# A turn ahead of the second pair of scores, behind the weighted sum, in a gated attention and expert kernel

## The chip, the core and the metric

The kernel runs on one core of one Trainium2 chip. The metric is the device time of one execution in microseconds, smaller is better. The engines are TensorE (PE in the rows, with PEld for its weight loads), VectorE (DVE), ScalarE (ACT), GpSimdE (POOL) and SyncE (SP). Each works through its own queue in the order of the program and waits for the others at semaphores.

## What is computed

Eight sequences of 512 tokens, 256 wide, attend to 1601 context rows with 16 heads of width 16; then each token goes through two of eight experts. The softmax of the attention runs over the queries, not over the context (`axis=2`), and the second division is by the sum over the context.

```python
def _L0_xattn_ref(q, k, v, Wq, Wk, Wv, Wo):
    scale = Dm ** (-0.5)
    qh, kh, vh = ...                        # heads of q @ Wq.T, k @ Wk.T, v @ Wv.T
    attn = jnp.einsum('bhnc,bhlc->bhnl', qh * scale, kh)
    attn = jax.nn.softmax(attn, axis=2)
    attn = attn / jnp.sum(attn, axis=-1, keepdims=True)
    out = jnp.einsum('bhnl,bhlc->bhnc', attn, vh)
    out = out.transpose(0, 2, 1, 3).reshape(Bq, Nq, Dm)
    return out @ Wo.T

x = x + jnp.tanh(g_xattn[0]) * _L0_xattn_ref(_layernorm(x, axis=-1), ctx_1024, ctx_1024, ...)
x = x + jnp.tanh(g_ffn[0]) * _L0_ffn_ref(_layernorm(x, axis=-1), router_w, w1, w2)
```

## The kernel before

**Stages.** A short start fills the first projections. Then eight attention batches follow one another from about 31 us to 1230 us of the span, and the expert stage takes the rest. The change touches the attention alone.

**Steps.** A batch has 52 steps (`STEPS`): four groups of four heads, by 13 tiles of up to 128 context rows (`LT`). A step `s` has two pairs of heads. For each pair TensorE makes two score tiles of 128x512 (`unit_scores(b, s, 0)` and `unit_scores(b, s, 1)`, L732), VectorE takes the negated maximum of both in one reduction (`negmax`, L1114), and ScalarE takes two exponentials with their sums (L934). I write scores(48,1) for the second pair of step 48, and the same for maxima and exponentials. The scores of a pair go into one of three slots of PSUM (`SLOTS`), so a pair has to wait for the exponentials of the pair three before it. Once the sums of a step are there, VectorE takes a reciprocal (L1100), GpSimdE scales the values (`vz`, L1337), and TensorE makes the weighted sum of the step three before the current one (`weigh(it.b, s - LAG)`, L745, four products of 32x512 that run side by side and add up in `acc`).

**Fills.** Between these, TensorE does the other work of the previous, current and next batch in pieces, one at certain steps, by the table `FILL_AT` (two more tables hold for the first and the last batch). Each piece goes into the one PSUM bank `spare`, and another engine takes it from there. Some are projections (`k`, `q`, `v`, `out_proj`) that are made in two halves, the first half at the step ahead of the table's. Others are turns, which are four transposes of 128x128 each: `o_turn` (L669), `attn_turn` (L672), `row_turn` (L684) and `x_turn` (L582). A piece waits until the one before it has left `spare` (`fill_taken`). VectorE takes `o_turn` with a reciprocal and a product (L1015, L1017) and `attn_turn` and `row_turn` with a copy (L1004); ScalarE takes `x_turn` (L883). VectorE's order within a step is written out: the maximum of the first pair, the taking of a turn, the maximum of the second pair, then the accumulator's copy if one is due (L1104), and the reciprocal of the step before.

**The order on TensorE.** In `run` of the TensorE block a step goes either of two ways. In the ordinary one the fill stands between the first and the second pair, and the weighted sum comes last. Where `begins_behind(s)` holds, which it does where the first half of a piece falls on the step behind another piece's end, the weighted sum goes ahead of the second pair, and the half behind it. The pads and prefixes of the routing and its small steps on VectorE do not matter here.

Of the kernel before, what the change touches and what calls it, by code (L numbers as in the profile page):

```python
# [78 lines left out]
    47: ("next", "v", 6), 48: ("cur", "attn_turn", 0), 49: ("cur", "o_turn", 2),  # L79
}  # L80
LAST_BATCH_FILL_AT = {**FILL_AT, 44: ("tail", "pads", 0)}
HALVED = ("k", "q", "v", "own_v", "out_proj")
LAST_V = (("v", VF - 1), ("own_v", VF - 1))

# [29 lines left out]
class Iteration:  # L114


    def __init__(self, b, tail=True, cur=True, nxt=True):
        self.b, self.tail, self.cur, self.next = b, tail, cur, nxt
        has = {"tail": tail, "cur": cur, "next": nxt}
        self.ahead = nxt and not (b + 2 >= B)  # L120
        self.table = FIRST_BATCH_FILL_AT if b == 0 else LAST_BATCH_FILL_AT if b == B - 1 else FILL_AT
        order = [self.table[s] for s in sorted(self.table) if has[self.table[s][0]]]
# [14 lines left out]
    def halves(self, s):  # L137

        now, after = self.fill(s), self.fill(s + 1)
        begun = after and after[0] in HALVED and after not in LAST_V  # L140
        assert not (begun and now) or now[0] in HALVED
        if now:
            split = now[0] in HALVED and now not in LAST_V
            return [(now, (1,) if split else (0, 1))]
        return [(after, (0,))] if begun else []

    def begins_behind(self, s):

        begun = any(halves == (0,) for _, halves in self.halves(s))
        return begun and self.fill(s - 1) is not None and (s - LAG) % LT > 0  # L150

    def chunk(self, name, i):
# [21 lines left out]
def wait(eng, sem, value):  # L174

    if not (isinstance(value, int) and value <= 0):
        eng.wait_ge(sem, value)
# [30 lines left out]
def rows_of(lt):  # L208
    return min(P, L - lt * P)


def attention_and_routing(nc, ctx, block, keep, x, ctx_t, g_xattn, g_ffn, wq_t, wk_t, wv_t, wo_t, router_t,
# [203 lines left out]
    def stacks_by(b, g):  # L416

        return b * LOADS - (LOADS if b > 0 and g == 0 else 0)
# [160 lines left out]
    def _(pe):  # L579
        def turn_x(bank, i):  # L580
            for t in range(NT):
                mm = pe.transpose(bank[:, t * P:(t + 1) * P], x_in[:, t, i * P:(i + 1) * P], ident[:, :])  # L582
            return mm

        def project_q(bank, i, halves):
            for k in halves:
                mm = pe.matmul(bank[:, :], wq_sb[:, k, i * P:(i + 1) * P], x_t[:, k, :], start=(k == 0), stop=(k == KC - 1))
            return mm

        def project_k(bank, i, halves):  # L590
            m, c = i // KCHUNK, i % KCHUNK
            for k in halves:
                mm = pe.matmul(bank[:, 0:KCOLS[c + 1] - KCOLS[c]], wk_sb[:, k, m * P:(m + 1) * P],  # L593
                               ctx_sb[:, k, KCOLS[c]:KCOLS[c + 1]], start=(k == 0), stop=(k == KC - 1))
            return mm

        def project_v(bank, i, halves):
            for lt in (2 * i + h for h in halves if 2 * i + h < LT):
                r = rows_of(lt)
                for k in range(KC):  # L600
                    mm = pe.matmul(bank[0:r, (lt % 2) * D:(lt % 2 + 1) * D], ctx_sb[:, k, lt * P:lt * P + r],  # L601
                                   wv_sb[:, k, :], start=(k == 0), stop=(k == KC - 1))
            return mm
# [39 lines left out]
        def fill(it, name, i, halves):  # L643
            b = it.b
            if 0 not in halves:
                pass
            elif name != "logits":

                wait(pe, fill_taken, it.made(name, i) - 1)
            if name == "x_turn":  # L650

                pe.wait_ge(xn_ready, 2 * (b + 2))
                mm = turn_x(spare, i)
            elif name == "q":
                mm = project_q(spare, i, halves)
            elif name == "k":
                if i == 0 and 0 in halves:
                    pe.wait_ge(ctx_loaded, (b + 1) * 16)
                mm = project_k(spare, i, halves)
            elif name in ("v", "own_v"):  # L660
                if (name, i) == ("own_v", len(EARLY_COPIED) - KC) and 0 in halves:

                    pe.wait_ge(early_copied, len(EARLY_COPIED))
                mm = project_v(spare, i, halves)
            elif name == "o_turn":

                pe.wait_ge(acc_taken, b * G + i + 1 if i < G - 1 else b * G)
                for t in range(NT):
                    mm = pe.transpose(spare[:, t * P:(t + 1) * P], o_acc[:, t * P:(t + 1) * P], ident[:, :])  # L669
            elif name == "attn_turn":  # L670
                for t in range(NT):
                    mm = pe.transpose(spare[:, t * P:(t + 1) * P], attn[:, t, i * P:(i + 1) * P], ident[:, :])  # L672
            elif name == "out_proj":
                if i == 0:
                    pe.wait_ge(wo_in, 32)
                for t in (2 * i + h for h in halves):
                    for k in range(KC):
                        mm = pe.matmul(spare[:, (t % 2) * D:(t % 2 + 1) * D], attn_t[:, k, t * P:(t + 1) * P],
                                       wo_sb[:, k, :], start=(k == 0), stop=(k == KC - 1))
            elif name == "row_turn":  # L680

                pe.wait_ge(rows_ready, 2 * b)
                for t in range(NT):
                    mm = pe.transpose(spare[:, t * P:(t + 1) * P], routed_rows[:, 0, t, i * P:(i + 1) * P], ident[:, :])  # L684
            elif name == "logits":
                for t in range(NT // 2, NT):
                    for k in range(KC):
                        mm = pe.matmul(spare[:, t * E:(t + 1) * E], row_t[:, k, t * P:(t + 1) * P],
                                       router_sb[:, k, :], start=(k == 0), stop=(k == KC - 1))
            elif name == "pads":  # L690
                mm = pe.matmul(spare[:, 0:E], ones[:, :], seen[:, :], start=True, stop=True)
            else:

                pe.wait_ge(route_step, b * ROUTE_STEPS)
                pe.matmul(spare[:, 0:NT * E], tri[:, :], chosen[:, :, :], start=True, stop=False)
                mm = pe.matmul(spare[:, 0:NT * E], ones[:, :], seen_at[:, :, :], start=False, stop=True)
            if 1 in halves:
                mm.then_inc(fill_ready, 1)
# [9 lines left out]
        def unit_scores(b, s, p):  # L708
            u = 2 * s + p
            g, lt = s // LT, s % LT  # L710
            if lt == 0 and p == 0:

                wait(pe, stack_in[g], stacks_by(b + 1, g))
                if b == 0 and g == 0:
                    pe.wait_ge(early_q_in, 16 * BLOCKS)
                    pe.wait_ge(early_k_in[0], 16 * BLOCKS)
            if b == 0 and g == 0 and p == 0 and lt == HALFWAY // P:
                pe.wait_ge(early_k_in[1], 16 * BLOCKS)

            emptied = 2 * (b * UNITS + (u - SLOTS if u >= SLOTS else (-2, -1, -3)[u]))  # L720
            if b == 0 and u < SLOTS:

                held = EARLY[u * 2 + 1 + BANKS_EARLY]
                if held in EARLY_SPLIT:
                    pe.wait_ge(early_split, EARLY_SPLIT.index(held) + 1)
                else:
                    pe.wait_ge(early_copied, EARLY_COPIED.index(held) + 1)
            for j in (2 * p, 2 * p + 1):
                r = rows_of(lt)

                wait(pe, exp_done, emptied + j % 2 + 1)
                mm = pe.matmul(scores[0:r, 2 * (u % SLOTS) + j % 2, :], k_stacks[g][:, j, lt * P:lt * P + r],  # L732
                               q_stack[:, g, j, :], start=True, stop=True)
            mm.then_inc(scores_ready, 1)
# [14 lines left out]
        def run(it):  # L749
            for s in range(STEPS):  # L750
                late = s >= LAG and it.cur and it.begins_behind(s)
                if it.cur:
                    unit_scores(it.b, s, 0)
                if late:
                    weigh(it.b, s - LAG)
                    unit_scores(it.b, s, 1)
                for f, halves in it.halves(s):
                    fill(it, *f, halves)
                if it.tail and s == LOGITS - 1:
                    first_logits(it)  # L760
                if it.cur and not late:
                    unit_scores(it.b, s, 1)
                    if s >= LAG:
                        weigh(it.b, s - LAG)
                if s < LAG and it.tail:
                    weigh(it.b - 1, STEPS + s - LAG)
# [63 lines left out]

        first()
        over_batches(pe, run)
        last()

# [854 lines left out]
```

## Time and profile before

| | |
|---|---|
| median of 3 runs | 1798.06 us (1796.43 to 1799.73) |
| the profiled execution's own time | 1794.36 us |
| its span in the profile | 1792.6 us |
| PE / DVE / ACT busy over the span | 95% / 79% / 72% |
| one attention batch, start to start | 151.3 us |
| busy in one such batch: ACT, DVE, PE | 148.63, 144.83, 143.79 us |

The shares over the whole span mix two stages: in the expert stage ScalarE has little to do and TensorE is the engine in front. In the attention all three are nearly full, so the question there is which one waits last, and that is read in the timeline, step by step. The granted TensorE clock is 1.00 of full speed in every attention batch. A busy ACT hides short stalls: the row of an exponential also covers the time in which it stood queued, and the distance between two starts tells more. It is 0.66 us where nothing holds ScalarE.

### The profile page before, as it was taken

What the parts mean: (1) busy time and instruction counts of PE and PEld (TensorE: products, weight loads), DVE (VectorE), ACT (ScalarE), POOL (GpSimd) and SP (SyncE); (2) the same over time, 40 slices, a digit from 0 to 9 for tenths busy, and PEclk for the clock granted to TensorE, in tenths of its full rate; (3) what the DMA queues carried; (4) which work ended last, traced back from release to release, by engine and by line L of the source; (5) the groups of instructions that cost most, each with busy time, mean ns of one, the idle gap of its engine ahead of it and who ended that gap; (6) DMA issues with size and microseconds to landing.
All of it is one profiled execution on the core that took longest, in us unless ns stands there. A gap on an engine that the chain in (4) does not pass through costs nothing.

```text
span 1792.6 us, 31795 instructions
## 1 busy us (share of the span) xinstructions
PE 1703.8 (95%) x10074; PEld 918.3 (51%) x10074; DVE 1417.2 (79%) x2293; ACT 1283.0 (72%) x3653; POOL 538.2 (30%) x821
## 2 busy tenths in 40 slices
PE   8999999999999999999999999889999999999997
PEld 5233334333333433333333342225899999999997
DVE  7998999999999999999999999997344444444442
ACT  5999999999999999999999999996111111111111
POOL 3331252352343225235223422213122222222222
PEclk9999999999999999999999999999999999999999
DMA  8546226414712721551371163419222222222221
GB/s 231 139 121 183 66 70 158 129 40 123 187 47 62 198 72 52 158 154 40 102 187 51 51 172 75 154 52 326 67 37 35 36 37 35 38 35 35 36 37 27
DMA packets 128247, 172.90 MB, mean 96 GB/s; under 512 B 14496, under 2 KB 105760, under 8 KB 128128
## 3 DMA queue, kind: packets, MB, share of 16 engines
q1 hardware_dynamic: 113152, 150.51, 30.8%
q0 software_dynamic: 14144, 20.44, 6.6%
q8 instruction: 54, 0.88, 0.2%
q14 instruction: 65, 0.53, 0.1%
q10 hardware_dynamic: 832, 0.53, 0.1%
HBM read 117.96 MB, written 53.47 MB: 96 GB/s over the span
## 4 chain that ended last, share of the span: by engine, by line
ACT 40%; PE 30%; DVE 20%; issue 7%; DMA 2%; POOL 1%; SPq 0%; POOLq 0%; DVEq 0%; ACTq 0%
ACT w_all L934 37%; DVE negmax L1114 14%; PE scores L1507 14%; PE scores L1520 13%; ACT w_all L879 1%; ACT parts L870 1%; DVE resid L1009 1%; DMA out<-row_t,gate_token 1%; PE spare L1497 1%; DVE rz L1100 1%; PE scores L732 1%; PE spare L593 1%; DVE x L1025 1%; DVE stats L1133 1%; DVE stats L1143 0%
## 5 line engine op out<-in xcount | busy, mean ns | idle before, releaser
L934 ACT ACTIVATE w_all<-scores,negmax 128x512 f32<-128x512 f32 (+1 forms) x1664 | 1128.9, 778 | 19.9 <-DVE negmax L1114 15.4
L1114 DVE TENSOR_REDUCE negmax<-scores 128x2 f32<-128x1024 f32 (+1 forms) x832 | 1001.9, 1215 | 53.8 <-PE scores L732 47.4
L732 PE MATMUL scores<-q_stack,w_all 128*128 128x512 bf16 (+1 forms) x1664 | 532.9, 385 | 42.1 <-ACT w_all L934 34.3
L934 ACT ACTIVATION_READ_ACCUMULATOR w_all<-scores,negmax 128x1 f32 (+1 forms) x1664 | 495.2, 298 | 0.0
L745 PE MATMUL acc<-w_all,vz 128*32 128x512 f32 (+1 forms) x3328 | 443.7, 605 | 0.0
L732 PEld LDWEIGHTS scores<-q_stack,w_all 128*128 128x128 bf16 (+1 forms) x1664 | 136.8, 99 | 575.2 <-ACT w_all L934 514.6
L1553 ACT ACTIVATE projections<-scores 128x512 f32<-128x512 f32 x142 | 84.8, 597 | 445.8 <-PE scores L1507 440.2
L1337 POOL TENSOR_TENSOR vz<-w_all,rz 128x68 f32<-128x68 f32 (+1 forms) x416 | 124.5, 299 | 776.3 <-DVE rz L1100 751.0
L1507 PEld LDWEIGHTS scores<-row_t,q_stack 128*128 128x128 f32 x2272 | 264.4, 192 | 7.0 <-issue 2.0
L1507 PE MATMUL scores<-row_t,q_stack 128*128 128x128 f32 x2272 | 265.6, 275 | 1.9 <-DVE row_t L1580 1.9
L1520 PE MATMUL scores<-room,projections 128*128 128x256 f32 x1136 | 256.8, 379 | 0.0
L1633 POOL DMA_INDIRECT out<-row_t,gate_token x71 | 120.3, 1694 | 407.9 <-DVE row_t L1593 374.3
L1520 PEld LDWEIGHTS scores<-room,projections 128*128 128x128 f32 x1136 | 210.4, 190 | 25.7
L1586 DVE COPY gate_token<-parts 128x2 f32<-128x2 f32 x71 | 12.0, 169 | 186.3 <-DMA out<-row_t,gate_token 186.3
L745 PEld LDWEIGHTS acc<-w_all,vz 128*32 128x32 f32 (+1 forms) x3328 | 65.6, 108 | 138.1 <-issue 121.9
L593 PE MATMUL spare<-w_all,projections 128*128 128x400 f32 (+1 forms) x228 | 97.7, 511 | 10.2 <-DVE resid L1009 10.2
L1593 DVE TENSOR_SCALAR row_t<-scores,gate_token 128x256 f32<-128x256 f32 x71 | 34.4, 484 | 88.0 <-PE scores L1520 88.0
L601 PE MATMUL spare<-projections,w_all 128*128 128x256 f32 (+1 forms) x400 | 103.1, 381 | 0.1
L1570 DVE COPY q_stack<-w_all 128x2048 f32 x71 | 86.9, 1225 | 6.4 <-issue 1.8
L1575 DVE COPY room<-w_all 128x2048 f32 x71 | 86.5, 1218 | 0.0
L601 PEld LDWEIGHTS spare<-projections,w_all 128*128 128x128 f32 (+1 forms) x400 | 73.6, 186 | 19.8 <-ACT w_all L879 3.3
L1100 DVE RECIPROCAL rz<-z 128x4 f32<-128x4 f32 (+1 forms) x416 | 69.7, 167 | 2.1 <-ACT w_all L934 2.1
(215 smaller groups left out, 1048.9 us busy)
## 6 DMA issues: line engine op xcount, KB each, us to landing
w_all<-k_parts SPq DMA_DIRECT2D x248, 200.1 KB, 3.5
w_all<-in_w SPq DMA_DIRECT2D x16, 1024.0 KB, 10.0
q_stack<-q_parts SPq DMA_DIRECT2D x248, 64.0 KB, 3.3
k_parts<-parts SPq DMA_DIRECT2D x42, 300.0 KB, 2.9
w_all<-in_ctx_t SPq DMA_DIRECT2D x7, 1601.0 KB, 7.1
parts<-routed SPq DMA_DIRECT2D x71, 129.0 KB
q_parts<-parts SPq DMA_DIRECT2D x14, 384.0 KB, 3.9
routed<-pad_row SPq DMA_DIRECT2D x8, 645.0 KB
```

The source lines that it names most:

```text
L593: mm = pe.matmul(bank[:, 0:KCOLS[c + 1] - KCOLS[c]], wk_sb[:, k, m * P:(m + 1) * P], ctx_sb[:, k, KCOLS[c]:KCOLS[c + 1]], start=(k == 0), ...
L601: mm = pe.matmul(bank[0:r, (lt % 2) * D:(lt % 2 + 1) * D], ctx_sb[:, k, lt * P:lt * P + r], wv_sb[:, k, :], start=(k == 0), stop=(k == KC ...
L732: mm = pe.matmul(scores[0:r, 2 * (u % SLOTS) + j % 2, :], k_stacks[g][:, j, lt * P:lt * P + r], q_stack[:, g, j, :], start=True, stop=True)
L745: mm = pe.matmul(acc[32 * j:32 * j + 32, :], vz[0:r, s % RING, j, :], probs[0:r, s % RING, j, :], start=(lt == 0), stop=(lt == LT - 1))
L934: act.activation(probs[0:r, s % RING, j, :], scores[0:r, 2 * (u % SLOTS) + j % 2, :], ACT.Exp, bias=negmax[0:r, u % 4, j % 2:j % 2 + 1], a ...
L1100: dve.reciprocal(rz[0:r, s % RING, :], z[0:r, s % RING, :]).then_inc(rz_ready, 1)
L1114: dve.tensor_reduce(negmax[0:r, u % 4, :], scores[0:r, 2 * (u % SLOTS):2 * (u % SLOTS) + 2, :], AX.X, ALU.max, negate=True).then_inc(negma ...
L1337: pool.tensor_tensor(vz[0:r, s % RING, :, 0:DH + 1], v_ones[b % 2][0:r, lt, g * GH:(g + 1) * GH, :], rz[0:r, s % RING, :].unsqueeze(2).to_ ...
L1507: mm = pe.matmul(ps_hidden[:, slot * BANKS + h // HB, (h % HB) * BLK:(h % HB + 1) * BLK], w1_sb[:, slot, k * HID + h * P:k * HID + (h + 1) ...
L1520: mm = pe.matmul(ps_y[:, slot, 0:D], hidden[:, slot, h * BLK:(h + 1) * BLK], w2_sb[:, slot, h * D:(h + 1) * D], start=(h == 0), stop=(h == ...
L1570: dve.tensor_copy(w1_sb[:, slot, :], w1_all[:, bass.ds(e * (KC * HID), KC * HID)]).then_inc(w1_ready, 1)
L1633: pool.indirect_dma_start(out=out, out_offset=bass.IndirectOffsetOnAxis(gate_token[:, slot, 1:2].bitcast(U32), 0), in_=result[:, slot, :], ...
```

## The change

A turn that stands directly behind another piece's step is now a reason for the second order too, and in such a step the turn goes behind the weighted sum and ahead of the second pair. At the old places of the second order, where no fill ends in the step, nothing changes: the second pair still goes ahead of the half.

```diff
+TURNS = ("o_turn", "attn_turn", "row_turn", "x_turn")
...
-        begun = any(halves == (0,) for _, halves in self.halves(s))
+        begun = any(halves == (0,) or f[0] in TURNS for f, halves in self.halves(s))
         return begun and self.fill(s - 1) is not None and (s - LAG) % LT > 0
...
                 if late:
                     weigh(it.b, s - LAG)
-                    unit_scores(it.b, s, 1)
+                    if not it.fill(s):
+                        unit_scores(it.b, s, 1)
                 for f, halves in it.halves(s):
                     fill(it, *f, halves)
+                if late and it.fill(s):
+                    unit_scores(it.b, s, 1)
```

This meets 70 steps: in each of the six middle batches steps 4, 5, 18, 19, 20, 27, 28, 33, 48 and 49; in the first batch 18, 27, 28, 33, 44 and 48; in the last one 5, 19, 20 and 49. No instruction is added or removed, and only TensorE's queue changes. The line numbers behind L146 move by one, so L732 becomes L733, and behind L753 by up to four.

On TensorE, steps 48 and 49 of the second batch before the change (L732 is a pair of scores, L745 a weighted sum, L672 and L669 the two turns):

```order
L732 MATMUL scores<-q_stack,w_all 128x512 x2
L672 MATMUL spare<-ident,room 128x128 x4
L732 MATMUL scores<-q_stack,w_all 128x512 x2
L745 MATMUL acc<-w_all,vz 32x512 x4
L732 MATMUL scores<-q_stack,w_all 128x512 x2
L669 MATMUL spare<-ident,o_acc 128x128 x4
L732 MATMUL scores<-q_stack,w_all 128x512 x2
L745 MATMUL acc<-w_all,vz 32x512 x4
```

And the same two steps after it, where L733, L746, L673 and L670 are the same four lines:

```order
L733 MATMUL scores<-q_stack,w_all 128x512 x2
L746 MATMUL acc<-w_all,vz 32x512 x4
L673 MATMUL spare<-ident,room 128x128 x4
L733 MATMUL scores<-q_stack,w_all 128x512 x4
L746 MATMUL acc<-w_all,vz 32x512 x4
L670 MATMUL spare<-ident,o_acc 128x128 x4
```

The weighted sum has moved ahead of the turn, and the second pair of a step now stands next to the first pair of the following one.

On TensorE, steps 18 and 19 of the same batch before (L669 is the `o_turn`, L684 the `row_turn`):

```order
L732 MATMUL scores<-q_stack,w_all 128x512 x2
L669 MATMUL spare<-ident,o_acc 128x128 x4
L732 MATMUL scores<-q_stack,w_all 128x512 x2
L745 MATMUL acc<-w_all,vz 32x512 x4
L732 MATMUL scores<-q_stack,w_all 128x512 x2
L684 MATMUL spare<-ident,routed_rows 128x128 x4
```

And after (L670 and L685 are the turns):

```order
L733 MATMUL scores<-q_stack,w_all 128x512 x2
L746 MATMUL acc<-w_all,vz 32x512 x4
L670 MATMUL spare<-ident,o_acc 128x128 x4
L733 MATMUL scores<-q_stack,w_all 128x512 x4
L746 MATMUL acc<-w_all,vz 32x512 x4
L685 MATMUL spare<-ident,routed_rows 128x128 x4
```

The same move: the turn that VectorE takes next stands one weighted sum further back. VectorE's, ScalarE's and GpSimdE's own rows are the same as before.

## Rows read from the trace of the kernel before

**Rows 1.** Busy time by engine in the fifth batch's stretch; us, instructions in brackets

```profile
634.49:785.79 151.30, 143.79 (x797) 51.21 (x797) 144.83 (x234) 148.63 (x436) 54.25 (x94) 1.00 0.39 108
```

**Rows 2.** Groups by line over six batches: count | busy us, mean ns | idle before

```profile
L934 ACT ACTIVATE w_all<-scores,negmax 128x512 f32<-128x512 f32 (+1 forms) x1249 | 848.0, 761 | 16.0 <-DVE negmax L1114 11.8
L1114 DVE TENSOR_REDUCE negmax<-scores 128x2 f32<-128x1024 f32 (+1 forms) x625 | 753.1, 1214 | 38.6 <-PE scores L732 34.6 <-issue 0.6
```

**Rows 3.** Timeline, steps 48 and 49 of the fifth batch: start us, duration us, instruction

```profile
771.84 0.61 PE L732 MATMUL scores<-q_stack,w_all 128*128 128x512 bf16 x2
...
772.28 0.60 PE L672 MATMUL spare<-ident,room 128*128 128x128 f32 x4
...
772.48 1.23 DVE L1114 TENSOR_REDUCE negmax<-scores 128x2 f32<-128x1024 f32 x1 [0.23 <-PE scores L732]
...
773.62 0.68 DVE L1004 COPY room<-spare 128x512 f32<-128x512 f32 x1
...
773.77 1.06 PE L745 MATMUL acc<-w_all,vz 128*32 128x512 f32 x8
...
774.77 0.60 PE L732 MATMUL scores<-q_stack,w_all 128*128 128x512 bf16 x2
...
776.55 0.25 DVE L1015 RECIPROCAL rden<-spare 128x16 f32<-128x16 f32 x1
...
777.18 1.22 DVE L1114 TENSOR_REDUCE negmax<-scores 128x2 f32<-128x1024 f32 x1
...
778.42 0.87 ACT L934 ACTIVATE w_all<-scores,negmax 128x512 f32<-128x512 f32 x1
```

**Rows 4.** Timeline of TensorE's weight loads at the attention's end

```profile
1228.07 0.16 PEld L745 LDWEIGHTS acc<-w_all,vz 128*32 128x32 f32 x8 [0.95 <-POOL vz L1337]
1229.07 0.52 PEld L780 LDWEIGHTS spare<-router_sb,ones 128*128 128x128 f32 x4 [0.84 <-issue]
```

**Rows 5.** Timeline, step 18 of the fifth batch

```profile
685.61 0.60 PE L732 MATMUL scores<-q_stack,w_all 128*128 128x512 bf16 x2
...
686.57 0.66 PE L669 MATMUL spare<-ident,o_acc 128*128 128x128 f32 x4 [0.36 <-DVE resid L1009]
...
687.06 0.59 PE L732 MATMUL scores<-q_stack,w_all 128*128 128x512 bf16 x2
...
687.56 0.25 DVE L1015 RECIPROCAL rden<-spare 128x16 f32<-128x16 f32 x1
687.59 0.16 PEld L745 LDWEIGHTS acc<-w_all,vz 128*32 128x32 f32 x8 [0.42 <-issue]
...
689.44 0.69 ACT L934 ACTIVATE w_all<-scores,negmax 128x512 f32<-128x512 f32 x1 [0.25 <-DVE negmax L1114]
```

**Rows 6.** Timeline, step 4 of the fifth batch

```profile
643.99 0.61 PE L732 MATMUL scores<-q_stack,w_all 128*128 128x512 bf16 x2
...
646.20 0.25 DVE L1015 RECIPROCAL rden<-spare 128x16 f32<-128x16 f32 x1
```

**Rows 7.** Timeline, step 33 of the fifth batch

```profile
728.40 0.60 PE L732 MATMUL scores<-q_stack,w_all 128*128 128x512 bf16 x2
...
730.84 0.24 DVE L1015 RECIPROCAL rden<-spare 128x16 f32<-128x16 f32 x1
```

**Rows 8.** Timeline, step 27 of the fifth batch, first scores and the second pair's exponential

```profile
710.58 0.61 PE L732 MATMUL scores<-q_stack,w_all 128*128 128x512 bf16 x2
...
715.20 0.79 ACT L934 ACTIVATE w_all<-scores,negmax 128x512 f32<-128x512 f32 x1
```

**Rows 9.** Timeline, step 44 of the first batch

```profile
155.19 0.60 PE L732 MATMUL scores<-q_stack,w_all 128*128 128x512 bf16 x2
...
156.98 0.25 DVE L1015 RECIPROCAL rden<-spare 128x16 f32<-128x16 f32 x1
```

**Rows 10.** Timeline, step 19 of the last batch

```profile
1138.68 0.60 PE L732 MATMUL scores<-q_stack,w_all 128*128 128x512 bf16 x2
...
1140.75 0.68 DVE L1004 COPY row_t<-spare 128x512 f32<-128x512 f32 x1
```

## The prediction

> **What bounds the kernel now.** I read the stretches by batch first, then the groups by line, then the timeline at the steps that the change meets. A middle batch lasts 151.30 us, and ScalarE is busy in 148.63 of it, VectorE in 144.83, TensorE in 143.79 [rows 1]. So ScalarE sets the pace, with 2.67 us to spare, and the two engines that feed it are almost as full. The groups say what it waits for: of 16.0 us idle before the exponentials of six batches, 11.8 ended with a maximum from VectorE [rows 2]. VectorE waits for scores, 34.6 us in the same six batches, and much of that costs nothing, since three slots of scores let it lag.
>
> The timeline shows which of these matters at a turn. VectorE's work runs back to back: in steps 48 and 49 the maximum from 772.48, the copy at 773.62, the reciprocal at 776.55 and the maximum from 777.18 stand in a chain without idle time (only the first row shows any, 0.23 us for the scores), and the exponential at 778.42 starts 0.02 us behind the end of the last, at 778.40 [rows 3]. At step 18 the exponential says it itself, 0.25 us idle until the maximum [rows 5]. So **at a step with a turn VectorE is the bound, and ScalarE waits for it**. Before the change VectorE never waits for a turn: neither the copies nor the reciprocals that take one show idle time ahead of them [rows 3, 5].
>
> **What the change does to that.** It takes nothing away. It moves the weighted sum ahead of the turn. Two things get later, the turn's result and the scores of the second pair, and one gets earlier, the first pair of the next step, which no longer has a weighted sum directly ahead of it.
>
> *How late the turn is.* I count from the first product of scores(s,0). The turn follows it at once by 0.44 us (771.84 to 772.28) and lasts 0.60, so its result is there at 1.04 [rows 3]. Now: a weighted sum starts 0.53 us behind its pair (687.06 to 687.59) [rows 5]. What follows a weighted sum starts its loads 1.00 us later, for scores (773.77 to 774.77) and for other f32 products alike (1228.07 to 1229.07) [rows 3, 4]. A turn whose first load isn't hidden lasts 0.66 us [rows 5]. And VectorE starts some 0.04 us behind a product's end: the scores at 771.84 last to 772.45, the maximum starts at 772.48 [rows 3]. Together 0.53 + 1.00 + 0.66 + 0.04 = 2.23; the finer starts of these rows make 2.22, and I take that.
>
> *When VectorE wants it.* That is the distance from scores(s,0) to the taking, in the rows of before. What lies between it and 2.22 is the delay, and since VectorE's chain behind it has no idle time before an exponential that already waits, the delay passes through to ScalarE.
> - Step 48, middle batches: 773.62 - 771.84 = 1.78, so the copy comes 0.44 late [rows 3]. The chain from there to the exponential at 778.42 has no gap, so it costs 0.44. Step 49's turn is then ready in time: scores(49,0) moves to some 774.2 (its own slot is emptied later, by 774.8, which holds the next weighted sum back), the turn is there at about 776.8, and VectorE wants it at 776.55 + 0.44.
> - Step 18: 687.56 - 685.61 = 1.95, late by 0.27, and the exponential at 689.44 already waits, so it costs 0.27 [rows 5]. Here the sum also fills the 0.36 us for which TensorE now waits for `spare`, which is why the turn is not later still. Steps 19 and 20 follow while VectorE is behind; their turns are ready 0.5 us before it wants them. Nothing more.
> - Step 4: 646.20 - 643.99 = 2.21, late by 0.01 [rows 6]. Step 5 follows VectorE's backlog, with 0.5 us to spare: 0.
> - Step 33: 730.84 - 728.40 = 2.44, ready 0.22 early: 0 [rows 7].
> - Steps 27 and 28: ScalarE takes these turns, and late. What counts is scores(27,1). It is done 2.02 + 0.60 us behind scores(27,0), so at 713.20; its maximum ends at 714.45, and the exponential isn't due before 715.20 [rows 8]. Margin 0.75: 0. Step 28 has about as much.
>
> The middle batches repeat to 0.01 us, so they give 6 x (0.44 + 0.27 + 0.01) = **4.3 us**.
>
> - The first batch: step 18 as above, 0.26. Step 44, wanted at 1.79, is 0.43 late [rows 9]; its exponential follows the maximum with 0.16 us of margin in the timeline, so 0.27 (0.43 at most). Step 48 has the distances of rows 3 and nearly no margin: 0.38. Together 0.9.
> - The last batch: step 19, wanted at 2.07, is 0.15 late [rows 10]; step 49, wanted at 2.04, 0.18; both are ahead of exponentials that already wait. Step 5 is covered by 0.1, and step 20 follows 19's lag. Together 0.3.
>
> *What gets earlier.* TensorE's queue is as long as before; at a step with a turn, 0.53 + 1.00 + 0.49 + 0.43 us against 0.44 + 0.49 + 0.53 + 1.00. The first pair of the next step comes earlier by at most a few tenths of a microsecond, until its slot is free. That helps only where VectorE waits for just these scores. Of its waits, behind all 70 steps, that is 0.8 us in sum, and these stand where ScalarE has margin. I take 0, with 0.8 us as the end on the side of a gain. Nothing else queues behind the moved sum: it waits for `vz` of three steps before, which GpSimdE has made a step earlier, and ScalarE and VectorE need its result a step later than they get it. No DMA moves.
>
> The sum is 4.3 + 0.9 + 0.3 = **+5.5 us**. Against the profiled execution's own 1794.36 that makes 1799.9; its time lies 3.7 us below the median of the three runs, 1798.06, and the forecast stands on the median: **1803.6 us**.
>
> **A rule against this sum.** The rows show no load between a weighted sum's last load and the next thing's, 0.84 us, whether scores or f32 products follow [rows 4]. The Trainium skill (TensorE: Matmul & The Clock Gate, section "Step-by-step: what each phase is for") says that TensorE may pull weight loads ahead of products in flight where row groups don't conflict or the load goes to the background buffer. By that rule the turn's load would lie under the sum; rows 4 disagree for what follows a weighted sum, and no row shows a turn in that place. It is the first rival below, and its price is from rows alone.
>
> **The rivals.**
> - *The turn starts as soon as the sum has streamed.* The eight products of a weighted sum last 1.06 us, and products of 512 columns that follow one another overlap by some 0.17 us, so a turn with its load hidden would start at 0.88 instead of 1.00 and last 0.60 instead of 0.66: ready at 2.04. Step 48 then costs 0.26, step 18 0.09, step 4 nothing: 6 x 0.35 = 2.1, and the ends 0.4. That is +2.5, or **1800.6 us**, within 0.2%. For it: loads do run ahead elsewhere (a turn directly behind scores lasts 0.60). Against it: both kinds of followers in the rows.
> - *The turn is later than I take it.* At a further 0.2 us, by which the steps at 48, 18 and 4 all grow and 33 stays just covered (margin 0.22), the sum is 6 x (0.64 + 0.47 + 0.21) + 1.5 + 0.7, so +10.1, or **1808.2 us**. For it: no row shows transposes behind a sum of four side by side. Against it: loads for f32 products start on time there.
> - *The other side: scores of the next step decide.* If VectorE's chain is longer only because the next first pair comes late, the change gains. It would decide from the point where VectorE idles ahead of the first maximum behind a turn step. The upper end of that is the 0.8 us above, so **1797.3 us**; for more, ScalarE's 16.0 us of idle time would have to hang on these scores [rows 2], and the rows show VectorE busy without a gap where they would have to show it waiting. A real gain of more than 0.2% by it has hardly a chance.
> - *The loss is given back.* A stall that ScalarE has later in the batch could shrink. Its biggest ones, around steps 0 and 12, follow from ScalarE's own exponentials and slots and so move along. **1798.1 us** if they all did.
> - That the change does nothing at all is excluded: the moved rows stand in TensorE's queue at 70 steps.
>
> **How the numbers follow.** "Faster" and "slower" begin at 0.2%, 3.6 us, about what a measurement of this kernel can tell from none. The forecast has 0.70, the early turn 0.13, the later turn 0.09, the loss given back 0.05, the gain 0.03. A spread of some 1.5 us of the runs lies on each, by the three runs shown. Slower is 0.70 + 0.09 less a tail of the forecast that stays under 3.6 us, 0.02, so 0.77. Same is 0.13 + 0.05 + 0.02, less 0.01 that falls out on the side of a gain, 0.19. Faster is 0.03 and that 0.01, 0.04. The range goes from 1799.9, most of the way to the early turn, to 1808.0, near the later one.
>
> **What would show it.** In the profile of the changed kernel VectorE's copy L1004 and reciprocal L1015 show idle time ahead of them that a turn ended: about 0.44 at step 48 and 0.27 at step 18 of each middle batch, some 5 us in all. A middle batch lasts 152.0 instead of 151.3 us, all of it at exponentials (18,1), (48,1) and (49,1). The turn's loads start 1.0 us behind the sum's. ScalarE's idle time ended by maxima grows. The expert stage stays as it is. I am wrong if the copy at step 48 starts as before relative to scores(48,0), if a middle batch stays at 151.3, or if exponentials of steps 27, 28 or 33 begin to wait.

## The result: slower by 0.14%, less than half of what was forecast

| | before | after |
|---|---|---|
| median of 20 runs each, us | 1796.64 (1792.31 to 1799.73) | 1798.38 (1795.59 to 1803.21) |
| the profiled execution's span, us | 1792.6 | 1795.7 |
| the fifth batch, start to start, us | 151.30 | 151.83 |

The ratio is 1.0014, 95% interval 1.0008 to 1.0021. That is +2.5 us, from +1.4 to +3.8; the two medians alone are 1.7 us apart. It is a loss, as forecast, but of less than the 0.2% from which I called it slower, and the median lies below my range of 1799.9 to 1808.0. A second set of runs of the same kernel gave nearly the same ratio: 1.0015, interval 1.0007 to 1.0024, which is +2.7 us, from +1.3 to +4.3.

The groups by line of the changed kernel, over the whole span (count | busy us, mean ns | idle before), against [rows 2], which is over six batches:

```profile
L938 ACT ACTIVATE w_all<-scores,negmax 128x512 f32<-128x512 f32 (+1 forms) x1664 | 1129.4, 761 | 20.8 <-DVE negmax L1118 15.4
L1118 DVE TENSOR_REDUCE negmax<-scores 128x2 f32<-128x1024 f32 (+1 forms) x832 | 1000.8, 1214 | 52.0 <-PE scores L733 46.4
```

ScalarE's idle time ended by maxima is 15.4 us, and so it was before the change, over the whole span. The equal totals hide two changes. Over the six middle batches it grew from 11.8 to 12.9 us, as forecast, and in the last batch it fell from 1.8 to 0.6, since TensorE's clock had fallen there in the profile of before (a wait of 1.22 us at the first exponential of step 1) and not in this one. The line that shows the cause is in the view of waits (engine, line waited for: us in total, times, longest), and it has no counterpart before:

```profile
DVE room L1008 <- PE spare L673: 2.5, 7, 0.4
DVE rden L1019 <- PE spare L670: 1.7, 8, 0.4
```

VectorE now waits for turns, 15 times (the shortest waits, in the last batch, don't enter this view). The copy L1008 waits at step 48 of seven batches, 0.36 us each. The reciprocal L1019 waits at step 18 of seven batches and once at step 44 of the first. The timeline of steps 48 and 49 of the fifth batch, where [rows 3] had none of it:

```profile
773.82 0.60 PE L733 MATMUL scores<-q_stack,w_all 128*128 128x512 bf16 x2
...
774.36 1.07 PE L746 MATMUL acc<-w_all,vz 128*32 128x512 f32 x8
...
775.35 0.66 PE L673 MATMUL spare<-ident,room 128*128 128x128 f32 x4
...
776.04 0.69 DVE L1008 COPY room<-spare 128x512 f32<-128x512 f32 x1 [0.36 <-PE spare L673]
...
777.87 1.19 DVE L1118 TENSOR_REDUCE negmax<-scores 128x2 f32<-128x1024 f32 x1
777.90 0.72 ACT L938 ACTIVATE w_all<-scores,negmax 128x512 f32<-128x512 f32 x1
```

From the first scores at 773.82 the turn's load comes at 1.53 and the copy at 2.22, as worked out; before the copy stood at 1.78. And step 18, where [rows 5] had the reciprocal 1.95 us behind the scores:

```profile
688.76 0.42 PEld L670 LDWEIGHTS spare<-ident,o_acc 128*128 128x128 f32 x4 [0.84 <-DVE resid L1013]
688.77 0.66 PE L670 MATMUL spare<-ident,o_acc 128*128 128x128 f32 x4
...
689.46 0.26 DVE L1019 RECIPROCAL rden<-spare 128x16 f32<-128x16 f32 x1 [0.19 <-PE spare L670]
...
691.35 0.69 ACT L938 ACTIVATE w_all<-scores,negmax 128x512 f32<-128x512 f32 x1 [0.52 <-DVE negmax L1118]
```

ScalarE's idle time there went from 0.25 to 0.52 us. So the turn is late as forecast, and ScalarE waits for it at step 18. What remained was why a whole batch is only 0.53 us longer when the terms made 0.72, and the kernel +2.5 instead of +5.5.

**A finer reading.** I laid the exponentials of both traces over each other, one by one, from the first of their batch. By their starts the fifth batch falls behind at (18,1) by 0.27 us, (48,1) by 0.19 and (49,1) by 0.22, in sum 0.69, and gets 0.19 back at the very next batch's first exponential. By their ends the loss at (48,1) is 0.00 and that at (49,1) 0.25. There is also a gain of 0.10 at step 12. So starts and ends tell different stories, and the experiments had to say which counts. The exponentials (48,1) and (49,1), before and then after the change:

```profile
775.71 0.92 ACT L934 ACTIVATE w_all<-scores,negmax 128x512 f32<-128x512 f32 x1
778.42 0.87 ACT L934 ACTIVATE w_all<-scores,negmax 128x512 f32<-128x512 f32 x1
```

```profile
777.90 0.72 ACT L938 ACTIVATE w_all<-scores,negmax 128x512 f32<-128x512 f32 x1
780.85 0.69 ACT L938 ACTIVATE w_all<-scores,negmax 128x512 f32<-128x512 f32 x1
```

Both start later within their batch and are recorded as shorter by 0.20 and 0.18 us. I use one measure for the experiments: the length of a middle batch, the distance between the first exponentials of two batches in a row. It repeats within about 0.02 us inside an execution, so it tells apart what the timed runs cannot.

### The profile page after: what moved, and what is told of

The parts are those of the page before. It is cut to its first block, busy times and chain, and to the rows that moved or that the text cites. A ratio compares the mean times of both kernels' runs of the same rounds, so it can differ in the third digit from the quotient of the medians.

```text
span 1795.7 us, 31682 instructions
## 1 busy us (share of the span) xinstructions
PE 1694.8 (94%) x9961; PEld 919.5 (51%) x10074; DVE 1417.1 (79%) x2293; ACT 1285.1 (72%) x3653; POOL 539.7 (30%) x821
## 4 chain that ended last, share of the span: by engine, by line
ACT 35%; PE 34%; DVE 21%; issue 7%; DMA 2%; POOL 1%; SPq 0%; POOLq 0%; DVEq 0%; ACTq 0%
ACT w_all L938 33%; DVE negmax L1118 14%; PE scores L1511 14%; PE scores L1524 13%; PE acc L746 2%; PE scores L733 2%; ACT w_all L883 1%; PE spare L594 1%; ACT parts L874 1%; DVE resid L1013 1%; PE spare L1501 1%; DVE rz L1104 1%; DVE stats L1147 1%; DVE x L1029 1%; DVE stats L1137 1%
## 5 line engine op out<-in xcount | busy, mean ns | idle before, releaser
L938 ACT ACTIVATE w_all<-scores,negmax 128x512 f32<-128x512 f32 (+1 forms) x1664 | 1129.4, 761 | 20.8 <-DVE negmax L1118 15.4
L733 PE MATMUL scores<-q_stack,w_all 128*128 128x512 bf16 (+1 forms) x1551 | 502.1, 384 | 69.4 <-ACT w_all L938 53.7
L938 ACT ACTIVATION_READ_ACCUMULATOR w_all<-scores,negmax 128x1 f32 (+1 forms) x1664 | 466.7, 280 | 0.0
L746 PE MATMUL acc<-w_all,vz 128*32 128x512 f32 (+1 forms) x3328 | 443.0, 605 | 0.0
L733 PEld LDWEIGHTS scores<-q_stack,w_all 128*128 128x128 bf16 (+1 forms) x1664 | 143.0, 99 | 565.1 <-ACT w_all L938 509.9
L746 PEld LDWEIGHTS acc<-w_all,vz 128*32 128x32 f32 (+1 forms) x3328 | 65.6, 108 | 133.2 <-issue 119.7
```

The lines of the kernel that those rows point to most:

```text
L746: mm = pe.matmul(acc[32 * j:32 * j + 32, :], vz[0:r, s % RING, j, :], probs[0:r, s % RING, j, :], start=(lt == 0), stop=(lt == LT - 1))
L938: act.activation(probs[0:r, s % RING, j, :], scores[0:r, 2 * (u % SLOTS) + j % 2, :], ACT.Exp, bias=negmax[0:r, u % 4, j % 2:j % 2 + 1], a ...
```

## The experiments

All kernels are the changed one with an edit to the rule or the order. For the six that only limit the steps, the rule gets one more condition, and `turned` names the steps, given below for the middle, the first and the last batch:

```diff
-        begun = any(halves == (0,) or f[0] in TURNS for f, halves in self.halves(s))
+        turned = s in (... if 0 < self.b < B - 1 else ... if self.b == 0 else ...)
+        begun = any(halves == (0,) or (f[0] in TURNS and turned) for f, halves in self.halves(s))
```

Two theories stood against each other. **The late turn:** VectorE waits for the turn, since a weighted sum is ahead of it. **The late second pair:** the scores of the second pair start later too, 2.24 us behind those of the first pair at step 48 instead of 0.94, and 2.03 instead of 1.45 at step 18, and VectorE or ScalarE waits for them. The traces at hand already speak against the second: over the six middle batches VectorE idles 33.2 us for scores before the change and 34.0 after it.

| kernel | middle batch, us | against 151.30 | ratio to before (95%) |
|---|---|---|---|
| after | 151.83 | +0.53 | 1.0014 (1.0008 to 1.0021) |
| e0_after_again | 151.75 | +0.45 | 1.0015 (1.0007 to 1.0024) |
| e1_covered | 151.52 | +0.22 | 1.0006 (0.9997 to 1.0015) |
| e2_exposed | 151.91 | +0.61 | 1.0022 (1.0011 to 1.0033) |
| e3_turn_sum_pair | 153.09 | +1.79 | 1.0064 (1.0051 to 1.0077) |
| e4_turn_last | 153.19 | +1.89 | 1.0071 (1.0049 to 1.0093) |
| e6_48_only | 151.54 | +0.24 | one run |
| e7_49_only | 151.55 | +0.25 | one run |
| e8_4_and_5 | 151.20 | -0.10 | 0.9995 (0.9986 to 1.0005) |
| e9_18_and_44 | 151.58 | +0.28 | one run |

The batch lengths leave out batches in which TensorE's clock fell, which have a paragraph of their own below.

**e0_after_again**, the changed kernel itself.

> The changed kernel itself once more. By the ends of the exponentials a middle batch is longer by 0.53 us (0.27 at step 18, 0.25 at step 49, less 0.10 around step 12), and that repeats. The first stage and the expert stage carry the rest of any difference between two profiles, up to a microsecond or so. If the time moves as the batches say, the attention brings 4.0 us: 6 x 0.53, some 0.4 for the first batch and 0.35 for the last one. The rival is that the batches' difference comes and goes from one execution to the next; then its middle batches are not 151.83 us.

Measured: 151.75 us, and nearly the same ratio. The terms repeat: by the ends of the exponentials +0.28 at step 18, -0.09 at step 12, and +0.26 at step 49, where the first trace has +0.25. In the first trace the delay also grows by 0.08 us between steps 19 and 48, at no single step; here it doesn't. That is the difference between 151.83 and 151.75, and its cause stays open.

**e1_covered**: `turned` is (4, 5, 19, 20, 27, 28, 33), (27, 28, 33), (5, 20).

> The changed order only at the turn steps where VectorE takes the turn late or ScalarE takes it: 4, 5, 19, 20, 27, 28 and 33 of the middle batches, 27, 28 and 33 of the first, 5 and 20 of the last. If the loss comes from VectorE waiting for the turn, nothing is lost here, and each middle batch gets shorter by up to 0.10 us, where TensorE's first pairs come earlier up to step 12: 151.2 to 151.3 us a batch, the kernel -0.6 to 0 us. If the loss comes from the late second pair, which is as late at all these steps, middle batches lengthen by several tenths of a us.

Measured: 151.52, outside what either theory said in its plain form. Laid over the trace of before, it has two differences: -0.09 at step 12, and +0.31 at exponential (19,1). The view of waits names the latter:

```profile
DVE row_t L1009 <- PE spare L686: 1.3, 6, 0.2
```

Step 19's turn was covered in my sum by the lag of step 18. Here step 18 has the old order and no lag, so at step 19 the turn is late by itself: scores at 54.09 and the copy at 56.02 in the fifth batch of before, measured from its first exponential, are 1.93 us apart, against 2.22. It is the late turn again, 0.29 by that sum and 0.31 measured, and all of it passes through: that exponential already waited 0.14 us for its maximum before, with a recorded duration of 0.69. Next to nothing is lost at 4 (0.02), 5, 20, 27, 28 and 33, though the second pair comes behind the weighted sum there too. That speaks against the second pair as the cause in the changed kernel.

**e2_exposed**: `turned` is (18, 48, 49), (18, 44, 48), (19, 49).

> The changed order only at steps 18, 48 and 49 of the middle batches, 18, 44 and 48 of the first, 19 and 49 of the last. If VectorE's wait for the turn is the cause, the whole loss is here: a middle batch 0.53 to 0.63 us longer than before (151.83 to 151.93), the kernel +3.5 to +4.5 us. If the late second pair is the cause, it is 3 of 10 steps of a middle batch and brings about a third of the changed kernel's loss, +0.2 us a batch.

Measured: 151.91, and 1.0022, or +4.0 us. The whole loss is at these three of ten steps, and 0.08 more than with all of them, since the gain at step 12 is missing. VectorE idles 32.9 us for scores over the six middle batches, less than the 33.2 of before, while each of these batches is 0.61 us longer.

**e3_turn_sum_pair**: at the 70 steps the turn, then the weighted sum, then the second pair.

```diff
                 if late:
-                    weigh(it.b, s - LAG)
-                    if not it.fill(s):
-                        unit_scores(it.b, s, 1)
-                for f, halves in it.halves(s):
-                    fill(it, *f, halves)
-                if late and it.fill(s):
+                    if it.fill(s):
+                        for f, halves in it.halves(s):
+                            fill(it, *f, halves)
+                    weigh(it.b, s - LAG)
                     unit_scores(it.b, s, 1)
+                if not (late and it.fill(s)):
+                    for f, halves in it.halves(s):
+                        fill(it, *f, halves)
```

> At the same 70 steps the turn goes first, as before the change, then the weighted sum, then the second pair. The turn is on time, the second pair as late as in the changed kernel. If VectorE's wait for the turn is the cause, almost nothing is lost: at step 48 the scores are done 2.6 us behind the first pair's start and wanted at 2.38, 0.2 late and under the 0.23 us of reserve of ScalarE; a middle batch 151.2 to 151.4 us, the kernel -0.5 to +1 us. If the late second pair is the cause, this is as slow as the changed kernel, 151.8 us a batch.

Measured: 153.09, over three times the changed kernel's loss. My expectation was wrong, and its exponentials, laid over those of before, say where: +0.62 at (4,1), +0.63 at (18,1), +0.59 at (33,1), +0.22 at (49,1) by starts. At 4, 18 and 33 the turn has to wait until `spare` is empty. In the changed kernel the weighted sum fills that wait; here it stands behind it. Step 18 of the sixth batch:

```profile
849.11 1.21 DVE L1119 TENSOR_REDUCE negmax<-scores 128x2 f32<-128x1024 f32 x1
849.25 0.42 PEld L670 LDWEIGHTS spare<-ident,o_acc 128*128 128x128 f32 x4 [0.85 <-DVE resid L1014]
...
849.84 1.07 PE L746 MATMUL acc<-w_all,vz 128*32 128x512 f32 x8
850.24 0.25 DVE L1020 RECIPROCAL rden<-spare 128x16 f32<-128x16 f32 x1
...
850.83 0.11 PEld L733 LDWEIGHTS scores<-q_stack,w_all 128*128 128x128 bf16 x2 [0.84 <-ACT w_all L939]
...
851.48 1.23 DVE L1119 TENSOR_REDUCE negmax<-scores 128x2 f32<-128x1024 f32 x1 [0.53 <-PE scores L733]
```

The turn is on time, and the reciprocal follows the maximum without a wait. But the scores start at 850.83, and the second maximum idles 0.53 us for them. Over the six middle batches VectorE idles 49.1 us for scores, of which some 3 us belong to two falls of TensorE's clock. So a late second pair can cost more than a late turn; in the changed kernel it doesn't, since there the scores follow the turn at once, and VectorE is busy with the turn until they are done (0.19 us ahead of the turn at step 18, none ahead of the maximum behind it). At step 48, where `spare` is free, this order costs nothing by the ends, as expected.

**e4_turn_last**: at the 70 steps the weighted sum, the second pair, then the turn.

```diff
                 if late:
                     weigh(it.b, s - LAG)
-                    if not it.fill(s):
-                        unit_scores(it.b, s, 1)
+                    unit_scores(it.b, s, 1)
                 for f, halves in it.halves(s):
                     fill(it, *f, halves)
-                if late and it.fill(s):
-                    unit_scores(it.b, s, 1)
```

> At the 70 steps the weighted sum goes first, then the second pair, then the turn, which is ready another 0.38 us later than in the changed kernel (2.60 us behind the first pair's start). If the wait for the turn is the cause, the copy at step 48 idles 0.82, the reciprocal at 18 0.65, at 4 0.39, at 33 0.16, and a middle batch is 1.4 to 2.0 us longer than before; the kernel +9 to +13 us. If the second pair's lateness is the cause, this mends most of it, since the second pair is 0.5 us earlier than in the changed kernel: below 151.8 us a batch.

Measured: 153.19, +1.89, inside the late turn's range and opposite to the other's. The waits for turns grew from 4.2 us in all to 14.6, of which these lines are 13.6:

```profile
DVE rden L1016 <- PE spare L670: 8.1, 21, 0.7
DVE room L1005 <- PE spare L673: 5.5, 8, 0.7
```

At (48,1) the start is 0.61 us late and the end 0.36.

**e6_48_only** and **e7_49_only**: `turned` is (48,) or (49,) in the middle batches, and none elsewhere.

> The changed order only at step 48 of the middle batches. The turn is 0.44 us late, and the lag stays in VectorE's chain up to exponential (49,1). If a waiting line of exponentials hides the first 0.2 us (their recorded duration has grown from 0.69 to 0.87 us by then, and falls back when ScalarE has to wait), a middle batch lengthens by 0.25 us. If the whole lag passes through, as I forecast, by 0.44.

> The changed order only at step 49 of the middle batches. Its turn is now late by 0.44 us by itself (wanted 1.78 us behind the first pair). With the line of exponentials as a reserve a middle batch lengthens by 0.25 us, as with step 48 alone and as with both; without it by 0.44, and both together would be no more than either.

Measured: 151.54 and 151.55, +0.24 and +0.25. The waits are there in full:

```profile
DVE room L1009 <- PE spare L674: 2.1, 6, 0.4
```

```profile
DVE rden L1020 <- PE spare L671: 2.1, 6, 0.4
```

That is 0.35 idle per batch, each a turn 0.44 us late, and 0.25 come out at the end. Each alone costs what both do in the changed kernel by the ends of step 49 (0.25 and 0.26), so it is one chain, not two losses.

**e8_4_and_5**: `turned` is (4, 5) in the batches after the first.

> The changed order only at steps 4 and 5 of the batches after the first. VectorE's reciprocal at step 4 comes 0.02 us late, and TensorE's first pairs come 0.1 us earlier up to step 12, where VectorE's chain holds ScalarE. A middle batch 0.08 to 0.12 us shorter, 151.2 us; the kernel -0.7 us, less than the timed runs can tell. If the gain around step 12 has another cause, 151.3.

Measured: 151.20, -0.10, as expected. The gain at step 12 repeats and comes from these two steps. For the kernel it is -0.6 us, and the ratio 0.9995 (0.9986 to 1.0005) can't tell that from nothing. It beats both kernels only by the batch's length.

**e9_18_and_44**: `turned` is (18,) in the middle batches, (44, 48) in the first.

> The changed order only at step 18 of the middle batches and at steps 44 and 48 of the first. Step 18 follows a stall of ScalarE at once, so its exponentials have no reserve (0.68 us each): the 0.27 us pass through in full, 151.57 us a middle batch. At 44 and 48 of the first batch the exponentials last over 1.0 us, a reserve of more than 0.3: their starts move by 0.29 and some 0.08 us, their ends do not, and the first batch stays at 149.25 us within 0.05, leaving out what its first steps may add by themselves. Without a reserve the first batch would be 0.6 us longer.

Measured: 151.58, +0.28, for step 18 alone. In the first batch the start of exponential (44,1) moved by 0.31 us and its end by 0.00, and the batch ends no later than that of before, but for 0.31 us at exponential (0,1), which other kernels with no change in this batch have too (e7 0.23, e8 0.31). The exponentials around step 44 of the first batch, before and then in e9, start and duration:

```profile
157.69 1.02 ACT L934 ACTIVATE w_all<-scores,negmax 128x512 f32<-128x512 f32 x1
158.35 1.02 ACT L934 ACTIVATE w_all<-scores,negmax 128x512 f32<-128x512 f32 x1
159.01 1.03 ACT L934 ACTIVATE w_all<-scores,negmax 128x512 f32<-128x512 f32 x1
```

```profile
157.63 1.04 ACT L939 ACTIVATE w_all<-scores,negmax 128x512 f32<-128x512 f32 x1
158.29 1.04 ACT L939 ACTIVATE w_all<-scores,negmax 128x512 f32<-128x512 f32 x1
159.26 0.74 ACT L939 ACTIVATE w_all<-scores,negmax 128x512 f32<-128x512 f32 x1
```

The third of each is (44,1). Its start went from 0.66 to 0.97 us behind the one ahead of it, its duration from 1.03 to 0.74: it ends at 160.04 and 160.00, and the ones ahead of it at 159.37 and 159.33. The start was late, the end was not. The rows overlap (157.69 and 1.02 reach to 158.71, and the next starts at 158.35). **An exponential here starts on record before it has the engine to itself, and the time that it stands in line is in its duration.** A delay of the start alone costs nothing here: the next batch comes later only by what the ends are late. So the line is a reserve: duration less the 0.68 us of one that follows a stall. It is 0.35 at step 44 of the first batch and 0.24 at step 48 of a middle one (0.92), where e4 has a start 0.61 late and an end 0.36 late. It is none at step 18, where the exponential had waited before too (0.69, [rows 5]).

## Why the prediction was wrong in size and right in mechanism

| term | forecast, us | measured, us |
|---|---|---|
| turn ready behind first scores | 2.22 | 2.22 |
| step 18, middle batch | 0.27 | 0.28 (e9) |
| steps 48 and 49 | 0.44 | 0.25 (after) and 0.26 (e0), by ends; 0.24 and 0.25 each alone |
| step 4 | 0.01 | 0.02 |
| steps 27, 28, 33 | 0 | 0 |
| step 12, from earlier first pairs | 0 (at most 0.8 in all) | -0.10 (e8) |
| first batch: 18, 44, 48 | 0.26, 0.27, 0.38 | 0.28, 0, 0 |
| last batch: 19, 49, starts | 0.15, 0.18 | 0.16, 0.19 |

**What bounds the kernel.** Right: ScalarE sets the pace, VectorE is late at turns, and before the change it never waited for one.

**How late the turn is.** Right to 0.01 us, and with it that nothing is loaded ahead behind the weighted sum. The early turn, my first rival, gave +2.5 us, and the timed runs gave +2.5. Yet its mechanism is refuted, as the load stands 1.53 us behind the scores in the changed kernel (773.82 to 775.35), not at 1.41. That the totals agree is chance.

**The step that failed** is "the delay passes through to ScalarE". I read margins from starts: the maximum at step 49 ended 0.02 us before its exponential started, so I took the whole 0.44 as lost [rows 3]. The rows had the answer in them. That exponential, at 778.42, has a duration of 0.87 where the one behind the stall at step 18 has 0.69 [rows 3, 5]. Those 0.18 us were reserve: 0.44 - 0.18 = 0.26, and 0.24 and 0.25 were measured. In the first batch the reserve covers both steps, and 0.65 us of my 0.9 were not there. I had written myself, under "Time and profile before", that an exponential's row also covers the time in which it stood queued, and did not use it in the sum.

**The second miss** is "I take 0" for what gets earlier. My bound of 0.8 us was right, and the value was not: behind steps 4 and 5 TensorE's first pairs come 0.1 us earlier up to step 11, VectorE starts its chain to exponential (12,0) earlier by it (34.28 to 34.18 us from the batch's first exponential in the two traces), and at (12,0) ScalarE has waited for VectorE all along. That is 6 x 0.10.

**The sum again**, with measured terms: 6 x (0.28 + 0.25 + 0.02 - 0.10) + 0.3 + 0.3 = 3.3 us. The attention itself, from its first exponential to its last and without the falls of the clock, is longer by 3.3 us in e0 and by 4.1 in the first trace. That trace has the slow growth described under e0 and another 0.2 us in its first batch, and what causes either stays open. The timed runs give 2.5, interval 1.4 to 3.8, and 2.7, interval 1.3 to 4.3. So 3.3 agrees with both, and 4.1, which is a single execution, with the second only. Between the two profiled executions the span differs by 3.1 us: 4.1 in the attention, less 1.14 for the fall of the clock in before, less 0.4 by which the attention starts earlier, and 0.5 more in the expert stage, which the change doesn't touch.

**The level it was added to.** A part of the distance to my 1803.6 us is no error of a term. I set the loss on 1798.06 us, the median of three runs; the median of 20 runs of the same kernel is 1796.64. That is 1.4 of the 5.2 us between forecast and measured median.

**The other rivals.** The later turn did not happen. That the loss is given back was right in part, and I had put it at 0.05: at the first exponential of the next batch 0.19 us come back by starts. I had said that such stalls move along with ScalarE. They do, but with its ends, and the ends had lost less. So nothing that counts is given back. That the next step's scores decide was right at one place, for -0.10 us a batch, and I had said that such waits stand where ScalarE has margin; at (12,0) it had none. The chances put 0.77 on slower by over 0.2%, and it was within 0.2%.

## What to carry to other kernels

Where an engine is the bound and its recorded instructions overlap, work out its margin from the ends: in this kernel the recorded duration less the duration of one behind a stall was slack that a late input used up at no cost. Before a long operation is put ahead of a short one whose result another engine takes, measure when that engine takes it; here the same move cost something at three of ten steps and next to nothing at the other seven, one of which (19) was covered only by the delay of the step ahead of it. And a wait for a free buffer is a place to put independent work into: at steps 4, 18 and 33 the weighted sum behind that wait cost 0.6 us a time, ahead of it 0.02, 0.28 and 0.

## What the runs showed of the hardware

**Durations on ScalarE grow while it is busy.** In the first batch the recorded duration of one kind of exponential goes from 0.69 to 1.15 us over the 52 steps with starts mostly 0.66 us apart, and falls back when one of them starts late. The distance between starts stays the same while the durations grow, so the engine isn't slower; the instruction's recorded start runs ahead of its service.

**The clock fell in the middle of a busy attention.** The rows of before for the start of the last batch (us, busy by engine, granted clock third from the end):

```profile
1085.00:1088.50 3.50, 2.06 (x12) 0.54 (x12) 2.04 (x4) 3.09 (x11) 1.29 (x2) 1.00 0.69 152
1088.60:1091.90 3.30, 3.30 (x16) 0.46 (x8) 1.93 (x3) 2.57 (x8) 0.29 (x1) 0.50 0.96 254
1092.00:1095.50 3.50, 3.33 (x22) 0.64 (x22) 3.50 (x5) 3.11 (x9) 0.30 (x1) 1.00 1.04 209
```

Ahead of it TensorE was busy 2.06 of 3.50 us. Then the granted clock is 0.50, which is 1.2 of 2.4 GHz, and back at 1.00 by 1092. So the sentence under "Time and profile before" that the clock is 1.00 in every attention batch holds for the six middle batches and not for the start of the last. The same happens around step 16 of middle batches, as in the third batch of e9:

```profile
374.70:378.10 3.40, 2.16 (x13) 0.37 (x11) 3.40 (x7) 3.40 (x12) 3.32 (x6) 1.00 0.02 5
378.20:381.50 3.30, 3.18 (x8) 1.01 (x12) 1.78 (x3) 2.69 (x9) 3.22 (x5) 0.50 0.51 168
```

The second batch of the same execution has the same quiet stretch at the same place and no fall, so that stretch by itself doesn't decide it:

```profile
223.10:226.50 3.40, 2.18 (x13) 0.37 (x11) 3.40 (x7) 3.40 (x12) 3.32 (x6) 1.00 0.00 0
226.60:229.90 3.30, 3.16 (x16) 1.22 (x17) 2.97 (x9) 3.20 (x10) 3.22 (x5) 1.00 0.50 167
```

Of eleven profiled executions nine have such a fall within the attention, 13 in all, and twelve of them begin 46.0 to 46.6 us behind the first exponential of their batch, at exponential (15,1); the changed kernel's first profile and e2's have none. One costs 1.14 us in the last batch and 1.55 to 1.65 us in a middle one (151.20 against 152.84 in e8). Which batches it meets differs from one execution of the same kernel to the next (one profile of the changed kernel has none, the other two). Two of them cost more than the whole change. They are a likely part of the spread of 7 us between runs of one kernel: of the changed kernel's 20 runs, the six with a mean granted clock of 0.997 have a median of 1796.6 us, and the four with 0.994 have 1802.0. The Trainium skill (TensorE: Matmul & The Clock Gate, section "Part 1: The HAM clock gate (the "warmup" mystery)") says that the clock has two levels and follows how busy TensorE has been; the levels agree with the 0.50 and 1.00 here, and the quiet stretches ahead of the falls fit, but no run here shows what decides in which batch it falls.
